# Reordering the matrix products of a decoder's attention passes on TensorE

## The chip, the cores and the metric
One core of a Trainium2 chip runs the whole kernel in one launch. The metric is the device time in microseconds (us), median of several executions. PE is TensorE (its weight loads are listed as PEld), DVE is VectorE, ACT is ScalarE, POOL is GpSimd, SP is the engine that issues the transfers, PSUM is the accumulator memory with eight banks of 128 x 512 words of 32 bits.

## What is computed
The input x is (2 sequences, 512 tokens, 128 channels). Six blocks follow, each `x = x + block(layernorm(x))`: attention (A), attention to a context with a top-32 choice (B), an FFN with 4-bit quantization (C), six layers of linear attention (D), attention to the context (E), and last six layers of local attention with an FFN (F), half of the kernel's time. Of F the reference says, cut to what matters:

```python
for i in range(6):
    x = attn_layer(shift_tokens(x), Wqkv[i], q_scale[i], k_scale[i], Wo[i]) + x
    x = ffn_layer(shift_tokens(x), ln_g[i], ln_b[i], W1[i], b1[i], W2[i], b2[i]) + x
# attn_layer: q, k, v = split(x @ Wqkv, 3), 16 heads of 64
#   q, k = l2norm(q) * qs, l2norm(k) * ksc; rotary tables on both
#   windows of 32: softmax(8 * q k^T, masked) v, each window sees itself and the one before
#   out @ Wo
# ffn_layer: layernorm; a, gate = split(xn @ W1 + b1, 2); (a * gelu(gate)) @ W2 + b2   (341 wide)
```

Block A has the same attention with one layer, its own mask width the same, and no l2 norm.

## The kernel before
Channels lie on the 128 partitions and the 512 tokens of a sequence along the free dimension, all in 32-bit floats. F is made of twelve units, one for each layer and sequence (b = 0, 1), and A of two. `attn_pe`, `attn_act`, `attn_dve`, `attn_pool` and `attn_sp` write the order of a unit out by hand, one for each engine; every engine works strictly in that order, and semaphores join them. A unit has three parts.

**Projection** (`a_head_pe`, `a_proj_pe`). The 16 heads are eight pairs p. For each, one product gives the queries (L285) and one the keys (L290), 128 x 512, into banks 0/1 and 2/3; ACT squares them (L485, L487), DVE multiplies them with the rotary tables (L603, L604, `a_rope_dve`), SP's transfers swap neighbouring partitions (L732), and POOL adds (L699, L700). Eight value products (L274, `a_v_pe`, i = 0 to 7) are spread over projection and first steps; ACT copies them out (L477). `a_ss_pe` (L329) sums squares for the l2 norm into bank 5. At the end ACT turns the sums into factors (guard L509, Ln L511, Exp L512), and two spreads (L337) bring the factors of pair 0 to all partitions, queries to bank 3 and keys to bank 2; those of the other pairs are bf16 products (L339). DVE multiplies the queries of a pair by its spread (`a_q_norm_dve`, L617; for pair 0 the keys too, L623); ACT copies the keys' spread (`a_k_norm_act`, L530) for POOL's multiply (L692).

**Steps** (`a_steps_pe`, p = 0 to 7). The mask is written into banks 0 and 1 by bf16 products (L370; L365 in step 7), the scores are added to it (L382), DVE takes maxima (L652) and subtracts (L655), ACT takes exponentials (L538), DVE sums the rows and inverts (L638, L645), POOL scales (L708), PE turns the result (L396, banks 4 and 5), ACT copies it out (L550), PE multiplies it with the values (L413, bank 6), ACT copies that out (L543), and the output product (L423) adds it up in bank 7. In the order of PE, step p has the mask and scores of p, the spreads of the queries of p+1 and the keys of p+2, the values of p-2, the turn of p-1 and the output product of p-3. ACT has in step p: copy of the key spread p+2, exponentials of p, merge of p-2, turned copies of p-1.

**Tail** (`a_tail_pe`). The last values, turn and output products, with the first products of the next unit's projection among them.

The FFN of a unit is done in the next unit's projection, through hooks by pair: `f_centre_pe` (L1886), `f_var_pe` (L1891), `f_up_pe` for i = 0, 1, 2 (gate L1899 in bank 6, up L1901 in bank 7), with i = 2 under the name "up", and `f_down_pe` (three products L1907, bank 7) under "down". ACT does the Gelu (L1957) and reloads the table of exponentials (L1961), DVE multiplies (`f_mul_dve`, L2003) and adds the result to x (L2008) after step 1. After step 3 DVE copies the shifted x, the source of the unit after the next, and in units of b = 1 it scales the rotary tables for the next layer (L2014) after step 5. `take(pe, k)` makes PE wait until bank k's last reader is done; `read` marks that. The last FFN has no next unit and runs alone at the end (`f_pe`).

## Time and profile before

| | us |
|---|---|
| median of 3 runs (lowest, highest) | 1825.26 (1824.89, 1825.85) |
| the profiled execution | 1826.93 |
| its span, first to last instruction | 1825.0 |
| busy: PE, DVE, ACT, POOL | 1598.0, 1211.4, 904.7, 583.9 |
| mean granted clock of PE, share of full speed | 0.938 |

The rows below are read so. A timeline row gives the start, the length from the first start to the last end, the engine and line, the operation, what it writes and reads, and how many instructions are merged; in brackets stand the time for which the engine had been idle and who released it. Products overlap at their ends, so the distance of two starts is the time that one takes from the engine. A 32-bit product of 128 x 512 is two instructions. A row of the table by stretches gives the busy time of each engine in a stretch. F runs from about 870 us to the end.

### The profile page before, as it was taken

Reading aid. Unit: us, or ns where it says so; the run is one execution under the profiler, and the core shown is the slowest. Engines: PE = TensorE matmul, PEld = TensorE weight load, DVE = VectorE, ACT = ScalarE, POOL = GpSimd, SP = SyncE. Lnnn points to the kernel's source line nnn. Section 1 sums busy time; section 2 is a strip of 40 time slices with the busy share of each in tenths; the row PEclk is TensorE's granted clock in tenths of the full one; section 3 lists DMA queues with packets and bytes.
Section 4 is the critical chain, followed back from the end, with each engine's and each line's share of the span. In section 5 each row is a group of like instructions: output and inputs, shape, how many; then the busy total and the mean of one; then the engine's idle time right before and its main releaser. Section 6 shows DMA issues by size and latency. Waiting matters only on the chain.

```text
span 1825.0 us, 37900 instructions
## 1 busy us (share of the span) xinstructions
PE 1598.0 (88%) x15445; PEld 865.5 (47%) x15445; DVE 1211.4 (66%) x2060; ACT 904.7 (50%) x1581; POOL 583.9 (32%) x546
## 2 busy tenths in 40 slices
PE   7877656999999998676899999999999999989996
PEld 2545324556556654221364454545546454453543
DVE  6685566556656564433777776877867787687773
ACT  2445322453444343223566566666666656656563
POOL 5461000000000000000556455465544646545461
PEclk9998567999999999677899999999999999999998
DMA  7130010000000000002313313142231422314120
GB/s 244 36 98 1 0 30 11 7 20 1 21 20 1 21 1 1 1 1 89 124 43 120 106 44 121 63 125 84 77 124 37 148 76 75 109 52 136 57 82 12
DMA packets 49514, 110.48 MB, mean 61 GB/s; under 512 B 15168, under 2 KB 20032, under 8 KB 48192
## 3 DMA queue, kind: packets, MB, share of 16 engines
q1 hardware_dynamic: 49344, 108.07, 18.2%
q8 instruction: 124, 2.03, 0.5%
q14 instruction: 46, 0.38, 0.1%
HBM read 28.61 MB, written 0.52 MB: 16 GB/s over the span
## 4 chain that ended last, share of the span: by engine, by line
PE 53%; DVE 27%; ACT 9%; issue 5%; DMA 2%; POOL 2%; SPq 1%; DVEq 0%; ACTq 0%
DVE nm L652 4%; PE ps L285 4%; PE ps L290 4%; DVE nm L638 3%; PE ps L1506 3%; PE ps L423 3%; PE ps L413 3%; PE ps L274 3%; PE ps L1557 3%; DVE big L655 2%; PE ps L1566 2%; PE ps L1525 2%; PE ps L396 2%; DMA big<-big 2%; DVE big L1750 2%
## 5 line engine op out<-in xcount | busy, mean ns | idle before, releaser
L699 POOL TENSOR_TENSOR big<-big 128x512 f32<-128x512 f32 x112 | 142.9, 1276 | 903.3 <-DMA big<-big 902.4
L708 POOL TENSOR_TENSOR big<-big,nm 128x384 f32<-128x384 f32 x224 | 189.4, 866 | 186.7 <-DVE nm L645 186.7
L603 DVE TENSOR_TENSOR big<-ps,big 128x512 f32<-128x512 f32 x224 | 153.7, 686 | 84.4 <-ACT sq L485 56.1
L538 ACT ACTIVATE big<-big 128x384 f32<-128x384 f32 x224 | 109.4, 522 | 126.1 <-DVE big L655 125.9
L604 DVE TENSOR_TENSOR big<-ps,big 128x512 f32<-128x512 f32 x224 | 152.6, 681 | 0.0
L413 PE MATMUL ps<-big 128*64 128x64 f32 x3584 | 129.1, 225 | 24.1 <-ACT big L550 23.8
L413 PEld LDWEIGHTS ps<-big 128*64 128x64 f32 x3584 | 115.1, 138 | 64.6 <-ACT big L550 47.5
L1750 DVE TENSOR_TENSOR big<-ps,fix 128x512 f32<-128x512 f32 x192 | 119.2, 683 | 36.4 <-PE ps L1506 36.0
L700 POOL TENSOR_TENSOR big<-big 128x512 f32<-128x512 f32 x112 | 143.1, 1277 | 0.0
L396 PE MATMUL ps<-ident,big 128*128 128x128 f32 x896 | 128.5, 282 | 14.5 <-POOL big L708 12.5
L692 POOL TENSOR_TENSOR big<-big 128x512 f32<-128x512 f32 x84 | 107.1, 1275 | 72.2 <-ACT big L530 72.1
L652 DVE TENSOR_REDUCE nm<-ps 128x4 f32<-128x384 f32 x224 | 112.2, 543 | 26.0 <-PE ps L382 23.5
L550 ACT ACTIVATE big<-ps 128x512 f32<-128x512 f32 x224 | 122.0, 593 | 9.4 <-PE ps L396 7.5
L477 ACT ACTIVATE big<-ps 128x512 f32<-128x512 f32 x112 | 66.6, 595 | 110.7 <-PE ps L274 110.7
L396 PEld LDWEIGHTS ps<-ident,big 128*128 128x128 f32 x896 | 96.8, 141 | 40.0 <-POOL big L708 26.9
L655 DVE TENSOR_TENSOR big<-ps,nm 128x384 f32<-128x384 f32 x224 | 113.5, 549 | 0.3
L638 DVE TENSOR_REDUCE nm<-big 128x8 f32<-128x768 f32 x96 | 91.5, 953 | 21.2 <-ACT big L538 19.5
L285 PE MATMUL ps<-xsh,big 128*128 128x512 f32 x192 | 101.6, 611 | 4.1 <-issue 4.1
L274 PE MATMUL ps<-big,xsh 128*128 128x512 f32 x192 | 103.9, 623 | 0.0
L382 PE MATMUL ps<-big 64*64 64x96 f32 (+1 forms) x3584 | 97.5, 244 | 5.8 <-DVE big L623 2.2
L423 PE MATMUL ps<-fix,big 128*128 128x512 f32 x192 | 99.6, 600 | 0.7 <-ACT fix L543 0.7
L290 PE MATMUL ps<-xsh,big 128*128 128x512 f32 x192 | 98.9, 597 | 0.0
(286 smaller groups left out, 2892.3 us busy)
## 6 DMA issues: line engine op xcount, KB each, us to landing
big<-big SPq DMA_DIRECT2D x224, 256.0 KB, 2.4
big<-big SPq DMA_DIRECT2D x112, 128.0 KB, 2.4
big<-in_F_w SPq DMA_DIRECT2D x6, 1536.0 KB, 6.7
big<-big SPq DMA_DIRECT2D x84, 64.0 KB, 2.0
big<-in_D_w SPq DMA_DIRECT2D x12, 256.0 KB, 2.9
big<-in_F_wo SPq DMA_DIRECT2D x6, 512.0 KB, 4.4
big<-in_F_w SPq DMA_DIRECT2D x6, 341.0 KB, 3.0
big<-in_A_w SPq DMA_DIRECT2D x1, 1536.0 KB, 11.1
```

The lines of the kernel that those rows point to most:

```text
L274: pe.matmul(ps[:, kv, :], src_of(key, b)[:, 128 * t:128 * t + 128], Wqkv[:, 2, 512 * hf:512 * hf + 512], start=True, stop=True).then_inc(* ...
L285: pe.matmul(ps[:, kq, :], Wqkv[:, 0, 128 * p:128 * p + 128], src_of(key, b), start=True, stop=True).then_inc(*full[kq].mark((key, b, "q", p)))
L290: pe.matmul(ps[:, kk, :], Wqkv[:, 1, 128 * p:128 * p + 128], src_of(key, b), start=True, stop=True).then_inc(*full[kk].mark((key, b, "k", p)))
L396: last = pe.transpose(ps[:, 4 + h, 128 * j:128 * j + 128], P[:, 2 * (p % 2) + h, at0:at0 + 128], ident[:, :])
L413: last = pe.matmul(ps[64 * h:64 * h + 64, 6, 64 * m:64 * m + 64], vv[:, m // 2, 128 * p + 64 * h:128 * p + 64 * h + 64], PT[:, 2 * (p % 2) ...
L423: last = pe.matmul(ps[:, Y, :], Wo[:, p, :], ot(key, p), start=p == 0, stop=p == NP - 1)
L603: dve.tensor_tensor(tmp[:, i, w, :], ps[:, k, :], tb[:, 2 * w, :], ALU.mult).then_inc(*part.mark((key, b, p, 0)))
L604: dve.tensor_tensor(sinp[:, i, T * w:T * w + T], ps[:, k, :], tb[:, 2 * w + 1, :], ALU.mult).then_inc(*part.mark((key, b, p, 1)))
L652: dve.tensor_reduce(nm[:, i, 4 * h:4 * h + 4], s4(h), AX, ALU.max).then_inc(*topped.mark((key, b, p, h)))
L655: dve.tensor_tensor(shft[:, 2 * (p % 2) + h, :].rearrange("p (j k) -> p j k", j=4), s4(h), nm[:, i, 4 * h:4 * h + 4].unsqueeze(2).to_broad ...
L708: pool.tensor_tensor(v, v, nm[:, p % 3, 16 + 4 * h:20 + 4 * h].unsqueeze(2).to_broadcast([128, 4, KW]), ALU.mult)\
L1750: dve.tensor_tensor(sT[:, ch % 2, r, :].rearrange("p (g i) -> p g i", g=4), ps[:, r, :].rearrange("p (g i) -> p g i", g=4), tri.unsqueeze( ...
```

## The change
PE's order is changed, and one bank; no product is added or removed, and ACT's, DVE's, POOL's and SP's orders stay. (1) `a_proj_pe`: the value product i = 5 goes ahead of the first two spreads, and the down products i = 0 and 1 behind them; the third down product goes into step 0. (2) `a_steps_pe`: the spreads stand between mask and scores from step 1 on (the key spreads of pairs 2 and 3 stay behind the value products of steps 0 and 1), and the hooks of a step ahead of those value products. (3) `a_tail_pe`: the next unit's first query product goes ahead of the values of pair 6, its first key product behind them, and the next two projections ahead of the output product of pair 6. (4) The third up product uses bank 2 in place of 7. Cut to its core:

```diff
@@ a_qk_pe is split: a_q_pe has the query product, a_k_pe the key product @@
+        def a_qk_pe(pe, key, b, p):
+            a_q_pe(pe, key, b, p)
+            a_k_pe(pe, key, b, p)
@@ a_proj_pe @@
                 a_ss_pe(pe, key, b, NP // 2 - 1)
-                a_v_pe(pe, key, b, 4)
+            a_v_pe(pe, key, b, 4)
+            a_v_pe(pe, key, b, 5)
+            if l2:
+                a_spread_q_pe(pe, key, b, 0)
+                a_spread_k_pe(pe, key, b, 0)
                 if "down" in hooks:
                     hooks["down"]()
-                a_spread_q_pe(pe, key, b, 0)
-                a_spread_k_pe(pe, key, b, 0)
-            else:
-                a_v_pe(pe, key, b, 4)
-            a_v_pe(pe, key, b, 5)
@@ a_steps_pe @@
                 a_mask_pe(pe, key, b, p, l2)
+                if l2 and p >= 2 and p + 2 < NP:
+                    a_spread_k_pe(pe, key, b, p + 2)
+                if l2 and 0 < p < NP - 1:
+                    a_spread_q_pe(pe, key, b, p + 1)
                 a_scores_pe(pe, key, b, p, l2)
-                if l2 and p + 1 < NP:
-                    a_spread_q_pe(pe, key, b, p + 1)
                 if l2 and p == 0:
+                    a_spread_q_pe(pe, key, b, 1)
                     a_spread_k_pe(pe, key, b, 1)
+                if p in late:
+                    late[p]()
                 if p < 2:
                     a_v_pe(pe, key, b, NT + 2 + p)
-                if l2 and p + 2 < NP:
-                    a_spread_k_pe(pe, key, b, p + 2)
-                if p in late:
-                    late[p]()
+                    if l2:
+                        a_spread_k_pe(pe, key, b, p + 2)
                 if p >= 2:
                     a_values_pe(pe, key, b, p - 2)
@@ a_tail_pe @@
+            if nxt:
+                a_q_pe(pe, *nxt, 0)
             a_values_pe(pe, key, b, NP - 2)
+            if nxt:
+                a_k_pe(pe, *nxt, 0)
             a_out_pe(pe, key, b, NP - 3)
-            if nxt:
-                a_qk_pe(pe, *nxt, 0)
             a_turn_pe(pe, key, b, NP - 1)
-            a_out_pe(pe, key, b, NP - 2)
             if nxt:
                 a_qk_pe(pe, *nxt, 1)
                 if v_with(l2, 1) is not None:
                     a_v_pe(pe, *nxt, v_with(l2, 1))
+            a_out_pe(pe, key, b, NP - 2)
             a_values_pe(pe, key, b, NP - 1)
@@ f_up_pe and f_mul_dve use bank UP[i] for the up product @@
+        UP = (7, 7, 2)
-            take(pe, 7)
-            pe.matmul(ps[0:m, 7, :], W1[:, c0:c0 + m], fxn, ...)
+            take(pe, UP[i])
+            pe.matmul(ps[0:m, UP[i], :], W1[:, c0:c0 + m], fxn, ...)
@@ f_down_pe @@
-        def f_down_pe(pe, l, b):
-            take(pe, Y)
-            for i, (c0, m) in enumerate(DIC):
+        def f_down_pe(pe, l, b, parts):
+            for i in parts:
+                if i == 0:
+                    take(pe, Y)
@@ f_pe_hooks: early, late (the epilogue calls f_down_pe with range(3)) @@
-                     "up": lambda: f_up_pe(pe, *u, 2), "down": lambda: f_down_pe(pe, *u)}, {})
+                     "up": lambda: f_up_pe(pe, *u, 2), "down": lambda: f_down_pe(pe, *u, (0, 1))}, {0: lambda: f_down_pe(pe, *u, (2,))})
```

## Rows read from the trace of the kernel before

**Rows 1.** The page, PE's busy tenths in 40 equal slices of the span
```profile
PE   7877656999999998676899999999999999989996
```
**Rows 2.** Table by stretches, one unit of each kind: stretch, length, busy by engine
```profile
1100.00:1177.00 77.00, 72.43 (x743) 37.98 (x742) 59.57 (x105) 48.04 (x85) 42.28 (x39) 1.00 0.29 95
1177.00:1255.00 78.00, 73.30 (x745) 38.35 (x744) 57.91 (x103) 48.50 (x86) 41.77 (x39) 1.00 0.27 88
```
**Rows 3.** PE's waits from 870 us on: total, times, longest
```profile
PE ps L413 <- ACT big L550: 19.9, 41, 1.1
PE ps L370 <- DVE big L655: 9.8, 22, 0.5
...
PE ps L1901 <- DVEq L136: 5.1, 5, 1.1
```
**Rows 4.** Timeline of PE, end of a projection and step 0, table unit
```profile
1129.50 2.74 PE L1907 MATMUL ps<-fix,big 128*128 128x512 f32 x6
1132.17 1.13 PE L337 MATMUL ps<-rs,big 32*128 32x512 f32 x4
...
1134.84 0.89 PE L382 MATMUL ps<-big 64*64 64x64 f32 x32 [0.20 <-DVE big L623]
...
1135.98 1.12 PE L274 MATMUL ps<-big,xsh 128*128 128x512 f32 x2
```
**Rows 5.** Timeline of ACT in the same unit
```profile
1128.87 0.69 ACT L509 ACTIVATE rs<-ps,eps 128x512 f32<-128x512 f32 x1
...
1130.43 0.72 ACT L512 ACTIVATE rs<-rs,eps 128x512 f32<-128x512 f32 x1
```
**Rows 6.** Timeline of PE, tail of the same unit, back-to-back products
```profile
1172.55 1.13 PE L423 MATMUL ps<-fix,big 128*128 128x512 f32 x2
1173.51 1.02 PE L285 MATMUL ps<-xsh,big 128*128 128x512 f32 x2
1174.37 1.02 PE L290 MATMUL ps<-xsh,big 128*128 128x512 f32 x2
```
**Rows 7.** Timeline of PE, step 4 of the table unit
```profile
1151.90 0.36 PE L370 MATMUL ps<-band,identb 64*64 64x384 bf16 x4
1152.09 0.83 PE L382 MATMUL ps<-big 64*64 64x64 f32 x32
1152.85 0.39 PE L339 MATMUL ps<-xn,big 32*128 32x512 bf16 x2
1153.16 1.15 PE L413 MATMUL ps<-big 128*64 128x64 f32 x32
```
**Rows 8.** Timeline of DVE in step 0 of the same unit
```profile
1135.76 1.02 DVE L652 TENSOR_REDUCE nm<-ps 128x4 f32<-128x384 f32 x2 [0.41 <-PE ps L382]
...
1139.31 0.95 DVE L638 TENSOR_REDUCE nm<-big 128x8 f32<-128x768 f32 x1 [1.00 <-ACT big L538]
```
**Rows 9.** Timelines of ACT and PE, end of a projection, plain unit
```profile
1207.56 0.69 ACT L509 ACTIVATE rs<-ps,eps 128x512 f32<-128x512 f32 x1 [1.13 <-PE ps L329]
...
1211.05 1.13 PE L337 MATMUL ps<-rs,big 32*128 32x512 f32 x4
```
**Rows 10.** Timelines of DVE and PE around step 3 of the table unit
```profile
1146.73 0.68 DVE L617 TENSOR_TENSOR big<-big,ps 128x512 f32<-128x512 f32 x1
...
1147.47 0.89 PE L382 MATMUL ps<-big 64*64 64x64 f32 x32
...
1148.51 0.97 DVE L652 TENSOR_REDUCE nm<-ps 128x4 f32<-128x384 f32 x2
```
**Rows 11.** Timeline of PE, values of pair 6, table and plain unit
```profile
1171.47 1.15 PE L413 MATMUL ps<-big 128*64 128x64 f32 x32 [0.67 <-ACT big L550]
...
1249.06 1.15 PE L413 MATMUL ps<-big 128*64 128x64 f32 x32 [1.13 <-ACT big L550]
```
**Rows 12.** Timelines of PE and DVE in the epilogue
```profile
1814.84 1.09 PE L1901 MATMUL ps<-xc,big 128*85 128x512 f32 x2
...
1816.83 2.84 PE L1907 MATMUL ps<-fix,big 128*128 128x512 f32 x6 [0.90 <-DVEq L136]
...
1819.71 0.75 DVE L2008 SCALAR_TENSOR_TENSOR x<-ps,big,x 128x512 f32<-128x512 f32 x1 [2.99 <-PE ps L1907]
```

More of the change, by code:

```diff
@@ L275, in a_v_pe, with a_q_pe @@
                       start=True, stop=True).then_inc(*full[kv].mark((key, b, "v", i)))
-        def a_qk_pe(pe, key, b, p):
-            kq, kk = p % 2, 2 + p % 2
+        def a_q_pe(pe, key, b, p):
             if p == 0:
@@ L281, in a_qk_pe, with a_k_pe @@
             if p < 2:
-                take(pe, kq)
+                take(pe, p)
             else:
                 pe.wait_ge(*q_part.at((key, b, p - 2, 1)))
-            pe.matmul(ps[:, kq, :], Wqkv[:, 0, 128 * p:128 * p + 128], src_of(key, b), start=True, stop=True).then_inc(*full[kq].mark((key, b, "q", p)))
+            pe.matmul(ps[:, p % 2, :], Wqkv[:, 0, 128 * p:128 * p + 128], src_of(key, b), start=True, stop=True).then_inc(*full[p % 2].mark((key, b, "q", p)))
+        def a_k_pe(pe, key, b, p):
+            kk = 2 + p % 2
             if p < 2:
@@ L1899, in f_up_pe @@
             pe.matmul(ps[0:m, 6, :], W1[:, DI + c0:DI + c0 + m], fxn, start=True, stop=True).then_inc(*full[6].mark(("F", l, b, "gate", i)))
[L1900 to L1905 removed]
+            take(pe, UP[i])
+            pe.matmul(ps[0:m, UP[i], :], W1[:, c0:c0 + m], fxn, start=True, stop=True).then_inc(*full[UP[i]].mark(("F", l, b, "up", i)))
+        def f_down_pe(pe, l, b, parts):
+            for i in parts:
+                if i == 0:
+                    take(pe, Y)
+                m = DIC[i][1]
                 pe.wait_ge(*f_mul.at((l, b, i)))
                 last = pe.matmul(ps[:, Y, :], W2[0:m, i, :], fh[0:m, i, :], start=i == 0, stop=i == 2)
[L1908 removed]
+            if i == 2:
+                last.then_inc(*full[Y].mark(("F", l, b, "f2")))
         def f_before(l, b):
@@ L1932, in f_pe @@
                 f_up_pe(pe, *u, i)
-            f_down_pe(pe, *u)
+            f_down_pe(pe, *u, range(3))
         def f_square_act(act, l, b):
@@ L2000, in f_mul_dve @@
             m = DIC[i][1]
-            dve.wait_ge(*full[7].at(("F", l, b, "up", i)))
+            dve.wait_ge(*full[UP[i]].at(("F", l, b, "up", i)))
             dve.wait_ge(*gg.at((l, b, i)))
-            dve.scalar_tensor_tensor(fh[0:m, i, :], ps[0:m, 7, :], b1[0:m, i:i + 1], fg[i % 2][0:m, :], ALU.add, ALU.mult).then_inc(*f_mul.mark((l, b, i)))
-            read(dve, 7, f_mul, (l, b, i))
+            dve.scalar_tensor_tensor(fh[0:m, i, :], ps[0:m, UP[i], :], b1[0:m, i:i + 1], fg[i % 2][0:m, :], ALU.add, ALU.mult).then_inc(*f_mul.mark((l, b, i)))
+            read(dve, UP[i], f_mul, (l, b, i))
         def f_add_dve(dve, l, b):
```

2 lines of the change are left out of this document (removed).

## The prediction
> **What bounds the kernel now.** I read the 40 slices of the page first: TensorE (PE) is at nine tenths or more in nearly every slice from the 21st on [rows 1], the last of the kernel's stages, which the change touches most. The table by stretches [rows 2] cuts that stage into its twelve units: 77 us for one of sequence 0 (a *plain* unit), 78 us for one of sequence 1 (a *table* unit, named for the scaling of the rotary table that VectorE does in it), with PE busy for 72.4 and 73.3. So at most some 4 to 5 us of each unit are waits of PE, about 50 us in all, and everything else that PE does is kept by the change. The list of PE's waits [rows 3] names them: the value products wait for ScalarE to bring the turned probabilities out of PSUM (19.9 us in 41 places), the masks for VectorE's subtraction (9.8), and 5 times the third "up" product of the FFN for a freed bank (5.1). Reading the timeline of one unit engine by engine then shows what sets the pace. The projection is a packed PE. In the steps it alternates: PE is packed in some of them, in a table unit VectorE has no gap from the row sum of step 0 to step 7, and ScalarE's evacuations pace the value products. That decides how to sum: an edit counts where it moves PE in the projection and the tail, and the row sum of step 0 in the steps.
>
> **Head of the steps.** Now: three down products, the two first spreads, the value product i=5, the mask, the scores [rows 4]. The spreads start at 1132.17 only because the down products (2.67 us) stand ahead of them; their operand is ready when ScalarE's exponential ends, 1130.43 + 0.72 = 1131.15 [rows 5]. In the new order product i=5 fills the time up to there (its bank is free at 1128.87 + 0.69 = 1129.56, and a product takes 0.86 [rows 6]), and the spreads start at 1131.2, 1.0 earlier. Behind them now stand 2.67 us to the scores, of which a wait for VectorE is about 0.35 (the mask alone takes 0.19 before unhindered scores [rows 7]). In the new order two down products take the place of one value product: 2.67 - 0.35 + 0.86 = 3.2. So the scores of step 0 start 0.5 earlier, and VectorE's first maximum with them.
>
> But the third down product, 0.86, now stands in step 0 ahead of value product i=6. ScalarE works in order: copy of i=6, copy of the second key spread, exponentials of step 0, and the row sum waits 1.00 for these [rows 8]; it comes 3.33 after the start of product i=6 (1135.98). So that product and the row sum come -0.5 + 0.86 = **0.4 later** in a table unit. VectorE had no gap from here on, so this is a loss, although PE itself has waits in this step that could hold the product: it fits PE's gaps but not ScalarE's queue.
>
> **Third up product in bank 2.** In the plain units of layers 1 to 5 it waits about 1.0 [rows 3]. Bank 2 was last read by the rotary multiply of pair 6, long before. Then the square sums come earlier, and ScalarE's guard activation, which idles 1.13 for them [rows 9], starts at 1206.43 after its table load. The spreads can follow 1131.2 - 1128.87 = 2.3 later, at 1208.8 instead of 1211.05: 2.3 earlier. With the same 0.5 and 0.86 behind them the row sum comes **0.9 earlier**. In table units nothing waited there.
>
> **Spreads behind the mask.** Work is moved, not removed: a pair of spreads takes 0.31, mask 0.19, scores 0.76 [rows 7]. The key spread can use the wait behind the mask. The query spread can't: it and the scores wait for the same VectorE multiply. In step 3 that ends at 1146.73 + 0.68 = 1147.41, and the scores start at 1147.47 [rows 10]; now the query spread's 0.31 comes between. The maxima of step 3 start at 1148.51 by VectorE; new by PE: 1147.47 + 0.4 + 0.31 + 0.92 = 1149.1 (0.92 from the start of scores to the maxima, [rows 4, 8]), so 0.2 more late than the 0.4. In steps 4 and 5 PE is packed, and the scores come 0.31 later against the same chain, while the values come no later. One more change of tile shape is added per step (mask, spread, scores; it was mask and scores together). [rows 6] give the nearest price: 0.96 from the output product, behind the values' other tile shape, to the query product, against 0.86 where the shape stays; so 0.10, between 0 (hidden, since the masks are short) and 0.2 (on either side); I take 0.10. No reason makes it a gain. Together the slip over the steps is 0.2 to 1.0; I take 0.6 in a table unit, where VectorE's table work hands the whole lateness on, and 0.35 in a plain unit, where PE gets the 0.31 back in step 6.
>
> The Trainium skill (TensorEngine Tiling (Array Packing), Key Properties) says that changing the tiling mode, not just the tile, drains TensorE. By this rule the extra changes are never free, and the trace agrees as far as it goes (0.96 against 0.86); no row shows a spread between mask and scores. Without it the sum would be about 1 us lower.
>
> **Tail.** The next unit's first query product, 0.86, goes ahead of the value product of pair 6, which waits 1.13 in a plain and 0.67 in a table unit [rows 11]. Its bank is free since VectorE's last subtraction (done before the output product ahead of it ends), its source since step 3. So it is hidden: **-0.86** plain, **-0.74** table (0.12 hangs over). The key product moved behind those values, the next queries ahead of the sixth output product: same work, and PE has no other wait there. Rotary work of pairs 0 and 1 starts earlier on VectorE, and SP issues these swaps earlier, but from pair 2 on it still follows the residual add. SP is passed no new DMA.
>
> **Last unit and epilogue.** It has no successor, so its tail keeps its wait: +0.4 + 0.35. In the epilogue the down products wait for the last multiply, since bank 7 is theirs and the third up product's: up at 1814.84, down at 1816.83, add at 1819.71 [rows 12]. With bank 2 the first two can start behind the up product, 1815.6; the third starts at 1817.3, and the add at 1818.4: **-1.3**.
>
> **The sum.** Five plain units with an FFN: 5 x (-0.9 + 0.35 - 0.86) = -7.0. Five table units: 5 x (0.4 + 0.6 - 0.74) = +1.3. First unit (no FFN, tail gain less slip) -0.5. Last unit +0.75. Epilogue -1.3. The first stage's tail is nearly without a wait: nothing. Sum -6.8. The profiled span is 1825.0 (that execution 1826.9); the median of the runs is 1825.26, so 1825.3 - 6.8 = **1818.5**.
>
> **Rivals.**
> *ScalarE's ring decides (slower).* The values of step p need the evacuation that ScalarE does behind the exponentials of step p-1. The new order puts the values right behind the scores, 0.31 closer, with 0.1 more for the tile shapes. If that ring is the bound in every step, two steps take 0.41 more, one 0.2, seven of them 1.4 per unit in place of my mean 0.5: 12 x 0.9 = +11, giving 1829.5. It decides from a slip of about 1.1 per unit (0.15 per step). For it: 41 waits on these evacuations; against: between them stand steps in which PE is packed without a wait (1151.90 to 1153.16 unbroken [rows 7]).
> *The freed bank is waited for again (no change).* The first key spread now stands behind the last FFN multiply, which reads bank 2. If that multiply comes late, the plain units lose their 1.3 again: 5 x 1.3 = 6.5, giving 1825. Against: even now, behind the wait of 1.0, that multiply is done before ScalarE's guard activation starts at 1207.56, and the spreads come later than 1208.
> *Everything fits the gaps (clearly faster).* If the third down product vanishes in step 0's gaps and no slip arises, 11 x 0.86 + 12 x 0.5 = 15 more: 1803. Against: ScalarE's order above.
> That the change doesn't do what it says holds for half of "spreads behind the mask" and is in the sum.
>
> **Chances.** Forecast 0.60, with its own range 1813 to 1823 (each term of a unit wrong by 0.4); ring 0.13; bank 0.14; all fits 0.13. The range takes in the forecast and the near half of the others: 1808 to 1828. A measurement can tell about 0.2% (3.7 us) from no change. Faster: 0.52 of the forecast and all of the last, 0.65. Same: 0.08 and the bank, with 0.01 of the ring: 0.23. Slower: 0.12.
>
> **What would show it.** Right: no wait of the third up product; the next query product ahead of the values of pair 6, and that wait gone or under 0.3; in step 0 VectorE's row sum waiting for ScalarE near 1.4 instead of 1.0; the query spread starting where VectorE's multiply ends. A plain and a table unit together, 155 now, near 153.9. Wrong: value products waiting 0.5 or more in most steps (ring), the first key spread waiting for VectorE (bank), or steps without PE waits at all.

## The result, and the profile after

| | before | after |
|---|---|---|
| median (lowest, highest) in the same session, us | 1826.23 (1824.5, 1829.32), 11 runs | 1831.06 (1827.59, 1840.46), 11 runs |
| ratio after to before | | 1.0036, 95% interval 1.0021 to 1.0050 |
| the profiled execution; its span | 1826.93; 1825.0 | 1828.03; 1826.2 |
| busy: PE, DVE, ACT, POOL | 1598.0, 1211.4, 904.7, 583.9 | 1611.0, 1224.9, 901.7, 584.9 |
| mean granted clock of PE | 0.938 | 0.935 |

The kernel became slower by 0.36%; 1818.5 was predicted, in a range of 1808 to 1828. It also became uneven: its runs spread over 13 us, those of before over 5. The profiled execution is one of the shortest of after: it lies 1.1 us above that of before, the medians lie 4.8 apart. In its code the two spreads of pair 0 are L342, the other spreads L344, the mask L375 (L370 in step 7), the scores L387, the turn L401, the values L418, the up product L1913, the down product L1921; on DVE the row sum is L648, the residual add L693, the shift copies L2002 and L2003.

**PE's waits** from 870 us on, after (compare [rows 3]):

```profile
PE ps L401 <- POOL big L718: 13.6, 11, 1.2
PE ps L418 <- ACT big L560: 8.5, 25, 1.0
PE ps L370 <- DVE big L665: 5.1, 5, 1.0
PE ps L342 <- ACT rs L522: 5.1, 12, 0.4
PE ps L375 <- DVE big L665: 3.7, 8, 0.5
...
PE ps L1896 <- DVE xsh L2003: 2.8, 5, 1.8
PE ps L387 <- DVE big L633: 1.8, 1, 1.8
...
PE ps L1913 <- DVEq L136: 0.4, 2, 0.2
```

The waits that the change aimed at are down: values 19.9 to 8.5, masks 9.8 to 3.7, third up product 5.1 to nothing (the 0.4 of the last line are waits of the second up product). Larger is the first line: 11 waits ahead of the turn of step 0, each of 1.24, where before has 0.52 (6.4 us in 12). But from 870 us to the end PE's idle time fell in all from 70.9 to 58.5 us, while its busy time grew by 13.6, from 884.1 to 897.7. So the list of waits doesn't show the loss, and the units have to be looked at one by one.

**Where the units changed.** The distance from the first spreads of one unit (L337 before, L342 after) to those of the next is a unit's period; it is read from the timeline of PE. *P* is the period from a plain unit to the table unit behind it (steps of the plain one, projection of the other), *T* the other one.

| period, us | before | after | the sum's working |
|---|---|---|---|
| first unit | 76.67 | 80.06 | 75.2 |
| T, five | 78.72 to 78.88 | 77.73 to 78.04 | 77.8 |
| P, five | 76.25 to 76.26 | 77.53 77.35 77.50 76.88 77.24 | 76.2 |
| last spread to the end | 72.66 | 71.56 | 73.1 |

The working is the sum's, cut at the spreads, which come 1.0 earlier in a table unit: so the first unit is 76.67 - 0.5 - 1.0, and the last stretch 72.66 + 0.75 + 1.0 - 1.3. The T periods came as worked out. The P periods are 5.5 us too long together, the first unit 4.9; these two make most of the error. The last stretch is 1.5 shorter, but it holds a piece at the lower clock in every trace, before's too (13.7 us there, 6.8 in after), so I take nothing from it.

**P periods: VectorE's copies.** Timelines of DVE and POOL in the tail of a plain unit, before:

```profile
1105.19 0.69 DVE L683 TENSOR_TENSOR x<-x,ps 128x512 f32<-128x512 f32 x1 [1.52 <-PE ps L423]
1106.02 0.42 DVE L1987 COPY xsh<-x 64x512 f32<-64x512 f32 x1
1106.48 0.42 DVE L1988 COPY xsh<-x 64x511 f32<-64x511 f32 x1
...
1106.67 1.37 POOL L699 TENSOR_TENSOR big<-big 128x512 f32<-128x512 f32 x1 [0.77 <-DMA big<-big]
```

and the same place after:

```profile
1107.35 0.69 DVE L693 TENSOR_TENSOR x<-x,ps 128x512 f32<-128x512 f32 x1 [2.25 <-PE ps L428]
1108.18 1.46 DVE L2002 COPY xsh<-x 64x512 f32<-64x512 f32 x1
1109.68 1.39 DVE L2003 COPY xsh<-x 64x511 f32<-64x511 f32 x1
...
1108.10 1.26 POOL L709 TENSOR_TENSOR big<-big 128x512 f32<-128x512 f32 x1 [0.75 <-DMA big<-big]
1109.33 1.46 POOL L710 TENSOR_TENSOR big<-big 128x512 f32<-128x512 f32 x1
...
1111.12 1.13 PE L1896 MATMUL ps<-xsh,fix 128*128 128x512 f32 x2 [0.24 <-DVE xsh L2003]
```

The copies take 1.46 and 1.39 in place of 0.42. It is so in three of the five P periods (77.53, 77.50, 77.24); in the other two the second copy alone is long, and the clock, below, has its part (77.35, 76.88). Before, the first copy started 0.65 ahead of POOL's rotary addition of the next unit's pair 1. Now VectorE's rotary work of pairs 0 and 1, which stands ahead of the residual add, is done 0.73 earlier against that add (DVE idles 2.25 before it in place of 1.52), the swaps and POOL's additions follow it, and POOL starts 0.08 *ahead* of the copy (0.65 - 0.73). Each copy then waits for the addition under way to end; the second addition, 1.46, waits in turn. PE's product L1896 is fed by the second copy. The Trainium skill (SBUF — State Buffer, SBUF: two separate sides) says that VectorE in a two-port mode and GpSimd arbitrate for one shared port pair, which is an exclusive lock held for the whole instruction; the trace agrees, with 0.42 against 1.39 to 1.46.

The kernel before already has such a pair in every unit behind the first, after step 3, where GpSimd's scaling starts 0.16 behind the first copy:

```profile
1152.11 0.37 DVE L1987 COPY xsh<-x 64x512 f32<-64x512 f32 x1
1152.51 0.94 DVE L1988 COPY xsh<-x 64x511 f32<-64x511 f32 x1
...
1152.27 1.86 POOL L708 TENSOR_TENSOR big<-big,nm 128x384 f32<-128x384 f32 x2 [0.75 <-DVE nm L645]
```

The second copy takes 0.94 in place of 0.42. The prediction had no row of it.

**The clock.** Table by stretches around step 0 of a plain unit, after; the last three columns are granted clock, DMA share, GB/s:

```profile
1215.00:1222.00 7.00, 6.85 (x85) 2.97 (x83) 4.43 (x9) 3.20 (x7) 2.54 (x2) 1.00 0.36 78
1222.00:1225.00 3.00, 1.78 (x14) 1.05 (x14) 3.00 (x7) 2.25 (x6) 2.79 (x3) 0.94 0.22 46
1225.00:1228.00 3.00, 3.00 (x56) 2.46 (x56) 2.41 (x6) 1.01 (x2) 2.25 (x4) 0.50 0.19 35
```

and PE there:

```profile
1223.09 1.44 PE L401 MATMUL ps<-ident,big 128*128 128x128 f32 x8 [1.24 <-POOL big L718]
1224.46 0.38 PE L375 MATMUL ps<-band,identb 64*64 64x384 bf16 x4
1224.78 0.61 PE L344 MATMUL ps<-xn,big 32*128 32x512 bf16 x2
1225.31 1.56 PE L387 MATMUL ps<-big 64*64 64x64 f32 x32
1226.80 1.71 PE L418 MATMUL ps<-big 128*64 128x64 f32 x32
```

Some 1.6 us after the end of the wait of 1.24 the clock falls to 0.50 of full speed, 1.2 GHz in place of 2.4, for 3.4 us, and 32 score products take 1.56 where they take 0.89 at full clock. This happened in three of after's eleven such units, one of them the last; in before, where this wait is 0.52, in none. In the first unit of after, which has no down products to put behind its first spreads, the same is larger. Timeline of PE:

```profile
899.14 1.13 PE L342 MATMUL ps<-rs,big 32*128 32x512 f32 x4 [0.42 <-ACT rs L522]
900.20 0.36 PE L375 MATMUL ps<-band,identb 64*64 64x384 bf16 x4
902.35 0.89 PE L387 MATMUL ps<-big 64*64 64x64 f32 x32 [1.79 <-DVE big L633]
904.08 0.70 PE L344 MATMUL ps<-xn,big 32*128 32x512 bf16 x2 [0.84 <-DVE xn L642]
904.72 2.07 PE L274 MATMUL ps<-big,xsh 128*128 128x512 f32 x2
```

The value product i=5, which filled the wait for VectorE, now stands ahead of the spreads. PE idles 1.79 and 0.84, and its clock is low from 903.8 to 914.1; before, only from 901.7 to 905.1.

### The profile page after: what moved, and what is told of

Its sections match the earlier page's. It is cut to its first block, busy times and chain, and to the rows that moved or that the text cites. A ratio compares the mean times of both kernels' runs of the same rounds, so it can differ in the third digit from the quotient of the medians.

```text
span 1826.2 us, 37900 instructions
## 1 busy us (share of the span) xinstructions
PE 1611.0 (88%) x15445; PEld 869.0 (48%) x15445; DVE 1224.9 (67%) x2060; ACT 901.7 (49%) x1581; POOL 584.9 (32%) x546
## 4 chain that ended last, share of the span: by engine, by line
PE 60%; DVE 20%; ACT 12%; issue 5%; POOL 2%; DMA 1%; SPq 0%; DVEq 0%; ACTq 0%; POOLq 0%
PE ps L292 4%; PE ps L418 4%; PE ps L284 4%; PE ps L428 4%; PE ps L401 3%; PE ps L1516 3%; DVE nm L662 3%; PE ps L274 3%; PE ps L1567 3%; PE ps L387 2%; PE ps L1576 2%; PE ps L1535 2%; PE ps L1921 2%; DVE big L1760 2%; PE ps L1911 2%
## 5 line engine op out<-in xcount | busy, mean ns | idle before, releaser
L613 DVE TENSOR_TENSOR big<-ps,big 128x512 f32<-128x512 f32 x224 | 153.8, 687 | 76.9 <-ACT sq L495 39.3
L548 ACT ACTIVATE big<-big 128x384 f32<-128x384 f32 x224 | 109.8, 522 | 159.3 <-DVE big L665 159.2
L401 PE MATMUL ps<-ident,big 128*128 128x128 f32 x896 | 127.4, 283 | 21.5 <-POOL big L718 19.7
L418 PE MATMUL ps<-big 128*64 128x64 f32 x3584 | 131.2, 227 | 13.5 <-ACT big L560 12.4
L418 PEld LDWEIGHTS ps<-big 128*64 128x64 f32 x3584 | 117.1, 140 | 47.7 <-ACT big L560 31.3
L401 PEld LDWEIGHTS ps<-ident,big 128*128 128x128 f32 x896 | 97.8, 142 | 44.9 <-POOL big L718 30.7
L487 ACT ACTIVATE big<-ps 128x512 f32<-128x512 f32 x112 | 66.4, 593 | 103.0 <-PE ps L274 103.0
L648 DVE TENSOR_REDUCE nm<-big 128x8 f32<-128x768 f32 x96 | 91.5, 953 | 33.4 <-ACT big L548 31.6
L387 PE MATMUL ps<-big 64*64 64x96 f32 (+1 forms) x3584 | 101.6, 250 | 1.9 <-DVE big L633 1.8
```

The source lines that it names most:

```text
L401: last = pe.transpose(ps[:, 4 + h, 128 * j:128 * j + 128], P[:, 2 * (p % 2) + h, at0:at0 + 128], ident[:, :])
L418: last = pe.matmul(ps[64 * h:64 * h + 64, 6, 64 * m:64 * m + 64], vv[:, m // 2, 128 * p + 64 * h:128 * p + 64 * h + 64], PT[:, 2 * (p % 2) ...
L613: dve.tensor_tensor(tmp[:, i, w, :], ps[:, k, :], tb[:, 2 * w, :], ALU.mult).then_inc(*part.mark((key, b, p, 0)))
```

## The experiments

Each ratio is to the kernel before on the same chip, with its 95% interval. Where a kernel has "additions", the shift in the tail is made by two additions from PSUM in place of the copies (those after step 3 stay). T and P are the periods of the profiled execution after the first unit. Since such a kernel's time scatters with the collisions, I read the time and the periods together. Each of the four groups below has its own runs of before: medians 1823.47, 1826.92, 1825.01 and 1826.48, the first two on one chip. So two ratios of one group compare well; the difference of two from different groups may be off by some 0.2%. Every trace has 3.4 to 13.7 us at the lower clock in the epilogue, and the last stretch is 68.2 to 73.0; no edit is behind this.

| kernel | ratio (95%) | P | T | wait ahead of the turn, total |
|---|---|---|---|---|
| after, again | 1.0076 (1.0060, 1.0091) | 76.2 to 78.0 | 77.7 to 80.5 | 13.6 |
| after, v5 late in first unit | 1.0075 (1.0060, 1.0090) | 76.5 to 77.9 | 78.6 to 81.0 | 14.5 |
| after, additions | 1.0030 (1.0019, 1.0042) | 76.1 to 76.8 | 78.0 to 79.8 | 13.6 |
| after, old tail | 1.0052 (1.0039, 1.0065) | 76.98 | 78.5 (one 79.0) | 13.7 |
| before, additions | 1.0003 (0.9994, 1.0012) | 76.26 | 79.2 to 79.4 | 6.5 |
| before, new tail | 1.0011 (1.0001, 1.0021) | 75.4, later 77.7, 78.2 | 78.0, later 79.0, 81.4 | 6.5 |
| before, new tail, additions | 0.9978 (0.9969, 0.9987) | 75.40 (one 76.2) | 78.6 (one 79.8) | 6.5 |
| the same with the freed bank | 0.9943 (0.9931, 0.9955) | 75.39 | 77.2 (one 78.2) | 6.4 |
| the same with the new head: all but the steps | **0.9912 (0.9900, 0.9924)** | 75.0 to 75.3 | 76.9 to 77.3 | 4.5 |
| all but the head, additions | 0.9972 (0.9962, 0.9982) | 75.8 to 76.1 | 77.7 to 78.7 | 6.6 |
| all, v5 late, additions | 0.9988 (0.9979, 0.9997) | 76.2 to 77.4 | 78.2 to 79.3 | 14.5 |
| the same, third down product in the head | 0.9988 (0.9980, 0.9997) | 76.12 (one 76.4) | 78.1 to 79.7 | 6.5 |
| the same, third down product behind i=6 | 0.9961 (0.9947, 0.9975) | 75.61 | 78.1 to 78.8 | 2.9 |
| after, third down product behind i=6 | 1.0019 (1.0007, 1.0031) | 75.67 | 77.9 to 80.4 | 2.1 |
| all but the steps, with the copies | 0.9952 (0.9940, 0.9965) | 75.04 or 76.17 | 77.3 or 79.1 to 79.4 | 4.5 |

### First group: the copies, the first unit, the tail

The kernel after unchanged, for the others to be compared with:

> The changed kernel once more, as it is: how its runs scatter, and whether what its first trace showed comes again. If the trace of the changed kernel is typical, this one has again the long shift copies on VectorE in the plain units' tails (1.4 us each in place of 0.42) and the low clock around 903 to 914 us, a ratio near 1.002 to 1.005, and units of 77.3 and 77.7 us. If the scatter of its runs (1827.6 to 1840.5, against 1824.5 to 1829.3 before) comes from the granted clock, this trace shows more or longer stretches at 1.2 GHz when its time is high. Rival: the scatter is the chip's own and the kernel before shows as much on the same chip.

1838.58 (1833.12 to 1839.12), ratio 1.0076. The kernel after has no single time: in this profile both copies are long in some *table* tails too (at 1188 and 1499), and just there the T periods are 80.00 and 80.45 in place of 78.

The value product i=5 behind the spreads again, in the unit without down products alone:

```diff
-            a_v_pe(pe, key, b, 5)
+            if not l2 or "down" in hooks:
+                a_v_pe(pe, key, b, 5)
             ...
                 if "down" in hooks:
                     hooks["down"]()
+                else:
+                    a_v_pe(pe, key, b, 5)
```

> The changed kernel, but in the first unit, which has no FFN work, value product i=5 goes back behind the first spreads. Theory (clock): without down products the changed order leaves TensorE idle for 1.8 and 0.8 us around the first scores, the granted clock falls to 1.2 GHz for some 10 us (903 to 914), and the first unit is 3.4 us longer than before (80.1 against 76.7 from spread to spread). Filled again, the first unit takes 76 to 77 and the whole is about 3 us shorter than the changed kernel. Rival: the low clock stems from what lies before it (the stage boundary), and comes whatever stands there; then under 1 us.

1837.5, ratio 1.0075. The first unit is 76.94 in place of 78.64 (80.06 in the first profile), so the mechanism is there; in the time it can't be seen, since the collisions scatter by more. For the time this run is inconclusive.

The shift without copies. The source x + y is read from PSUM, where the output product adds up y; nothing is left out:

```diff
@@ cut: the waits and marks are left out @@
+  dve.tensor_tensor(xsh[0:64, b, :], x[0:64, T*b:T*b + T], ps[0:64, Y, :], ALU.add)
+  dve.tensor_tensor(xsh[64:128, b, 1:T], x[64:128, T*b:T*b + T - 1], ps[64:128, Y, 0:T - 1], ALU.add)
-            late[NP + 2] = lambda: f_shift_dve(dve, l, b)
```

> The changed kernel, but VectorE makes the shifted x behind the tail as two additions from PSUM and x (both 0.69 us) in place of two copies within SBUF (0.42 alone, 1.4 when GpSimd adds at the time). The value is the same. Theory (collision): the changed tail brings GpSimd's rotary adds under these copies in plain units, two copies cost 2.0 us more there, and TensorE gets about 1 us of it as waits in the next projection. Without copies no collision: VectorE's part is 1.4 in every unit, against 0.84 undisturbed and 2.9 disturbed; the plain units take 76.3 to 76.8 from spread to spread, the table units 77.7 to 78.2, and the whole is 2 to 5 us shorter than the changed kernel. Rival: TensorE's own order (spreads, tile shapes) makes the plain units long; then no gain, or a loss of 0.5 us per unit.

1828.99, ratio 1.003, 9.6 us under the kernel after on the same chip, where I had expected 2 to 5. The undisturbed P periods are 76.14 and 76.17, what the sum's working gave. T is 78.0 to 79.8; two of the long ones hold a fall of the clock to 1.2 GHz, a third (79.03) a wait of 0.79 of the second up product. So the copies are a cause, not the only one. The edit does two things: the shift reads PSUM, and it stands ahead of the residual add, some 0.8 earlier. No kernel has one without the other. That an operation with a PSUM operand isn't stopped is seen in VectorE's rotary multiplies: they take 0.68 with a GpSimd addition under way (1260.47 and 1260.24 in the last kernel of the fourth group).

The kernel after with the old tail:

```diff
-            if nxt:
-                a_q_pe(pe, *nxt, 0)
             a_values_pe(pe, key, b, NP - 2)
             ... (the rest of a_tail_pe as before)
```

> The changed kernel with the tail of before (next query product behind the values of pair 6, next queries behind the output product). By the sum of the prediction the tail gave 0.86 and 0.74 per unit, so this should be about 9 us slower than the changed kernel. Theory (collision): it takes the collision away with the gain, since the first two rotary passes and their swaps come later again; then VectorE's shift copies are 0.42 long, and it is slower by only 0.8 x 11 - 1.0 x 6 = 3 us or less.

1833.12, ratio 1.0052, *less* than the kernel after in this group (1.0076), though not than its first result (1.0036). All its tail copies take 0.42, and P is an even 76.98. In after the new tail thus loses through the copies about what it gains, here more. But 1.0052 is well over 1: something else in the change costs as well.

### Second group: the tail on the kernel before

The control, before with the additions:

> The kernel before, with its two shift copies replaced by two additions that read the down sum from PSUM (0.69 us each instead of 0.42; nothing is left out). It is the control for the kernels that have the same edit. Collision theory: in the kernel before the copies run free (0.42 us) in the tails, so nothing is won; ratio to before 0.999 to 1.001. Rival, that the form of the shift is worth something by itself whatever the order of the passes: 0.995 or less, the same 9 us that it gave on the kernel after.

Ratio 1.0003: the form of the shift is worth nothing by itself (T is even 0.4 longer, since an addition takes 0.69 and a copy 0.42).

Before with the new tail alone (only `a_tail_pe` and the split of `a_qk_pe`):

> The kernel before with the new tail alone (query product of the next unit ahead of the late values). Collision theory: the 0.86 us per unit that the tail's working gives are there, but the copies of the plain units rise from 0.42 to about 1.4 us and give about 1.1 us back in those units; 1818 to 1824, ratio 0.997 to 1.000, plain-to-table periods no shorter than 76.3. Rival, head and steps are what made the kernel slower and the tail is clean: both kinds of period fall by 0.8, 1815, ratio 0.9955.

Ratio 1.0011. I had expected at most 1.000. The first unit has both copies long (78.15 in place of 76.67). Behind it P is 75.4 and T 78.0, 0.86 and 0.8 less than before, with the tail copies at 0.42 but for the second one in two P periods (1.38 and 1.40), which costs nothing there. From 1489 us on both copies are long in three of the last four tails that have a successor (1.38 to 1.48 and 1.39), in the third of the four the second alone, and the periods go up to 81.35, 78.19, 78.95, 77.66. One and the same program gains 0.8 in a unit or loses 2, by which of two engines comes first.

The same with the additions:

> The kernel before with the new tail, and with the shift as two additions from PSUM, so that no copy is there to be stopped. Collision theory: the tail's 0.74 to 0.86 us per unit arrive whole, periods 75.5 and 78.1, about 8 us in all: 1815 to 1817, ratio 0.9955. Rival, that the new order of the tail costs elsewhere (a PSUM bank, ScalarE, the residual add): same as before, ratio 1.0.

1823.97, ratio 0.9978. P is 75.40, by 0.86 under the control's 76.26, to the hundredth what the tail's working gave; T falls by 0.7. The gain in time, 0.25% of 1827 or 4.6 us against the control, is smaller than the 7.8 of the undisturbed periods; a wait of 1.4 of the second up product in one unit (T 79.80), one of 0.58 in the next and a longer slow stretch at the end (13.7 us in place of 6.8) take some of it.

The kernel after with both suspected causes taken away:

> The kernel after with both suspected causes taken away: the shift as two additions from PSUM, and in the first unit, which has no down products, the last value product back behind the spreads. If the two causes add, it lies 1.6 to 3 us under the kernel with the shift alone (ratio 1.003): 1821 to 1824, ratio 0.999 to 1.001, first unit 76.9 instead of 78.5. Rival, the first unit's slow clock is paid by something else: ratio stays 1.003. What neither covers is step 0's single wait of 1.24 us ahead of the turn (0.52 before): if a long wait there lets the clock fall, some units stay at 79.5 with granted clock 0.98 and others at 78.0 with 1.00.

1825.55, ratio 0.9988; first unit 75.71. Still four units in which the clock falls, each behind the wait of 1.24. The ratio is 0.42% under that of the additions alone, the median 3.4 us, the first unit 2.8 (78.50 before): the rest of the 0.42% lies in the two groups' runs of before. The tail alone on the kernel before does no worse (0.9978). So head, bank and steps together, without a collision, gave *nothing*, where I had expected gains from the head and the bank. Two long T periods (79.30, 79.05) have no fall of the clock but a wait of 1.29 and 1.04 of the second up product; the fourth group comes back to it.

### Third group: which part of head, bank and steps

New tail and freed bank, head and steps as before, additions:

```diff
-        UP = (7, 7, 7)
+        UP = (7, 7, 2)
```

> The kernel before with the new tail, the freed bank for the third up product, and the shift as two additions from PSUM; head and steps as before. If the bank removes the waits of the third up product (9.1 us over F with the tail and the shift alone, ratio 0.9978) and nothing takes their place, 1816 to 1819, ratio 0.994 to 0.996. If the down products wait in its place, 0.9978 stays. Step 0's wait ahead of the turn stays 0.52 us, and no unit after the first shows a granted clock of 0.98.

1814.26, ratio 0.9943. T falls from 78.55 to 77.20, which is the 1.3 that I had worked out for the bank.

All but the head (old steps' counterpart):

> The kernel after with the old head (all three down products ahead of the spreads, last value product behind them) and the shift as two additions; steps, tail and bank are new. Theory that the third down product in step 0 lengthens what stands between the scores of pair 0 and those of pair 1, and so makes one wait of 1.24 us ahead of the turn after which the clock falls: here the wait is 0.5 to 0.8 us, no unit shows 0.98, 1819 to 1822, ratio 0.996 to 0.998. Rival, the new order of the steps makes the wait: it stays at 1.2 and some units show 0.98, ratio 0.999 to 1.001.

1820.5, ratio 0.9972. The wait ahead of the turn is 0.52, no clock fall: as the theory had it. But the new steps cost 0.29% against the kernel above (P 0.4 to 0.7 and T 0.5 to 0.8 longer, but for one T).

All but the steps. The order of `a_steps_pe` is that of before, the third down product is in step 0 as in after, but by that old order it stands *behind* the value product i=6 and the key spread:

> The counterpart: new head with the third down product in step 0, old order of the steps, last value product of the first unit behind the spreads, shift as two additions, new tail and bank. Theory that the head makes the long wait: it is 1.2 us or more here as well, some units show a granted clock of 0.98 and are 1.5 us longer, 1823 to 1826, ratio 0.998 to 1.000. Rival, the steps make it: wait of 0.5 to 0.8, no such unit, ratio 0.995 to 0.997.

1809.85, ratio 0.9912, P 75.02, no clock fall after the first unit. Waits of 1.24 are gone here as well, so neither the new head nor the new steps makes them alone: it takes the third down product in step 0 *and* an order that puts it ahead of i=6. The expected size was wrong too: this is the fastest kernel of the study, 15 us under before (1825.01 on that chip).

Third down product back in the head, all else as in the kernel with 0.9988:

```diff
-  "down": lambda: f_down_pe(pe, *u, (0, 1))}, {0: lambda: f_down_pe(pe, *u, (2,))})
+  "down": lambda: f_down_pe(pe, *u, (0, 1, 2))}, {})
```

> Both causes taken away as in the kernel with ratio 0.9988, and the third down product back in the head with the other two, so that step 0 has 0.86 us less to fill its wait. Theory that the clock falls by chance after a long single wait: the wait ahead of the turn rises from 1.24 to about 1.6 to 2.1 us and more units show 0.98 than the four of that kernel; the head is 0.86 longer, the wait 0.86 longer only if the scores of pair 1 do not move; 1826 to 1832, ratio 1.000 to 1.003. Rival, the wait follows the scores of pair 1, which come 0.86 earlier after the spreads: the wait stays 1.24 or falls, and the time stays at 0.9988 or under it.

Ratio 0.9988 again. I had expected the wait to grow; it fell to 0.52, with another of 0.43 ahead of the mask of pair 1, and the turn comes 10.58 behind the first spreads as in the other kernel. The step waits about the same time in either place; only its cut into one wait or two differs. One fall of the clock is left, in step 7, and the ratio is no better though the four behind the turn are gone.

What stands between the orders shows on ACT and DVE. Step 0 of a plain unit in the kernel with 0.9988, timelines of ACT and DVE (here L490 is the copy of value product i=6, L551 the exponentials, L651 the row sum):

```profile
1213.92 0.60 ACT L490 ACTIVATE big<-ps 128x512 f32<-128x512 f32 x1 [1.29 <-PE ps L274]
1214.63 0.60 ACT L543 ACTIVATE big<-ps 128x512 f32<-128x512 f32 x1
1215.13 0.93 ACT L551 ACTIVATE big<-big 128x384 f32<-128x384 f32 x2
...
1216.09 0.95 DVE L651 TENSOR_REDUCE nm<-big 128x8 f32<-128x768 f32 x1 [1.86 <-ACT big L551]
```

and in the one with 0.9912 (L487, L548, L648):

```profile
1208.43 0.60 ACT L487 ACTIVATE big<-ps 128x512 f32<-128x512 f32 x1 [0.43 <-PE ps L274]
1209.14 0.60 ACT L540 ACTIVATE big<-ps 128x512 f32<-128x512 f32 x1
1209.63 0.93 ACT L548 ACTIVATE big<-big 128x384 f32<-128x384 f32 x2
...
1210.59 0.95 DVE L648 TENSOR_REDUCE nm<-big 128x8 f32<-128x768 f32 x1 [1.00 <-ACT big L548]
```

ACT waits for the value product (1.29 against 0.43), the exponentials queue behind that copy, the row sum behind them: 0.86 all the way, the time of the third down product.

### Fourth group: the third down product, the spreads, the copies

The edit to `a_steps_pe`, in both of the first two kernels:

```diff
-                if p in late:
-                    late[p]()
                 if p < 2:
                     a_v_pe(pe, key, b, NT + 2 + p)
                     if l2:
                         a_spread_k_pe(pe, key, b, p + 2)
+                if p in late:
+                    late[p]()
```

> As the kernel with both suspected causes taken away (0.9988), and in step 0 the third down product behind the value product i=6 and its key spread instead of ahead of them; the steps keep the spreads behind the mask. Theory that ScalarE's order carries the third down product into the row sum: its copy of product i=6 starts 0.86 earlier, the row sum's wait falls from 1.86 to about 1.0 us, PE's single wait ahead of the turn from 1.24 to 0.3 to 0.5, no unit shows a granted clock of 0.98, and 11 times 0.87 go: 1811 to 1815, ratio 0.992 to 0.9945. Rival, it is the spreads behind the mask that cost (0.9988 against 0.9912 of the kernel with the old steps): 0.997 to 0.9988, with the wait's length changed or not.

1819.38, ratio 0.9961, between the two theories. PE's waits ahead of the turn, over all of F:

```profile
PE ps L404 <- POOL big L726: 2.9, 12, 0.9
```

The waits there fall from 14.5 to 2.9 in all, the clock never falls between the first and the last unit, and P goes from 76.18 to 75.61. So the place of the third down product is worth 0.27%, 5 us. The rest, 0.9961 against 0.9912, is the spreads behind the mask: 9 us. P is 0.59 longer for them and T 1.2, and PE's busy time in a P period is 73.70 in place of 72.66. Where it goes is seen in a step in which PE never waits, here step 4 of after (compare [rows 7]):

```profile
1155.78 0.36 PE L375 MATMUL ps<-band,identb 64*64 64x384 bf16 x4
1156.07 0.39 PE L344 MATMUL ps<-xn,big 32*128 32x512 bf16 x2
1156.39 0.89 PE L387 MATMUL ps<-big 64*64 64x64 f32 x32
1157.21 1.15 PE L418 MATMUL ps<-big 128*64 128x64 f32 x32
```

From the mask to the values it is 1.43 in place of 1.26: 0.10 more at the mask (0.29 for 0.19) and 0.06 more at the scores (0.82 for 0.76). Six steps have this, so my estimate is 1.0 of busy time, which is the 1.04. The lateness against the first spreads adds up, 0.16 at the values of step 2, 0.33 at those of step 4, 0.58 at those of step 6, and that is the 0.59 of P. In a T period VectorE hands on 0.8 at step 7's mask, and the other 0.4 is the second up product, which waits 0.67 in place of 0.21.

> The kernel after with that one move alone (third down product behind the value product i=6); the copies on VectorE stay, the first unit stays as in the kernel after. If ScalarE's order is a term of the loss beside the copies, about 9 us go of the 6 to 14 that after lies above before: 1821 to 1828, ratio 0.997 to 1.001, with the copies still at 1.4 us in the plain tails and some units 2 us longer for it. If the copies decide alone, it stays at 1.004 to 1.008.

1829.62, ratio 1.0019. That is between my two expectations (up to 1.001, from 1.004). It gives something to the kernel after as well, and P is an even 75.67. The T periods split cleanly: 80.24, 80.44, 80.18 where both copies are long, 77.94 and 78.24 where both are free.

All but the steps with the two copies of before (edit of the third group, without the additions):

> The kernel with ratio 0.9912 (old steps, new head, tail and bank, first unit's last value product behind the spreads), but with the shift as the two copies of the kernel before. It prices the stopped copies on a base that is otherwise clean: collision theory, copies of 1.4 us in the plain tails and in some table tails, 6 to 12 us more than with the additions, ratio 0.995 to 0.998. Rival, on this base the copies meet no addition of GpSimd: 0.991, and then the additions from PSUM are not needed.

1819.17, ratio 0.9952. That prices the collision: 0.40%, 7.3 us. Timeline of DVE in two table tails, the first free, the second stopped:

```profile
1334.79 0.42 DVE L2002 COPY xsh<-x 64x512 f32<-64x512 f32 x1
1335.25 0.42 DVE L2003 COPY xsh<-x 64x511 f32<-64x511 f32 x1
...
1488.30 1.39 DVE L2002 COPY xsh<-x 64x512 f32<-64x512 f32 x1
1489.73 1.39 DVE L2003 COPY xsh<-x 64x511 f32<-64x511 f32 x1
```

T is 77.3 with the free pair and 79.4 with the stopped one, 2.1 more; P is 75.04 and 76.17, 1.1 more. In a P period with the stopped pair PE's product L1896 and the query and key products behind it start 0.34, 0.69 and 1.03 later against the spreads. In a T period half of the price comes another way, as PE's second up product shows in the same two units:

```profile
1353.57 1.12 PE L1913 MATMUL ps<-xc,big 128*128 128x512 f32 x2 [0.62 <-DVEq L136]
...
1509.15 1.13 PE L1913 MATMUL ps<-xc,big 128*128 128x512 f32 x2 [1.65 <-DVEq L136]
```

It waits for bank 7, which VectorE's multiply of the first one frees, and that multiply stands in VectorE's queue behind rotary work which waits for GpSimd's additions (2.44 in the second unit, 1.56 in the first). So this wait is 1.4 to 1.9 in ten of the eleven T periods with a stopped pair. In the kernels with additions it is there too, 0.8 to 1.6 in their long T periods without a fall of the clock, but for one of 77.27 (0.59). In *late_behind* each P period has only the second copy long (1.38) and is 75.67, against 75.61 with the additions: in P one stopped copy fits, two do not. In T it need not fit: 78.95 for 78.0 in the new tail alone.

## Why the prediction was wrong

**The step that failed** is the sentence on the tail, "Rotary work of pairs 0 and 1 starts earlier on VectorE, and SP issues these swaps earlier, but from pair 2 on it still follows the residual add". It was true and priced at nothing. I followed the earlier work on VectorE and SP and not on to the engine behind them: POOL's additions moved 0.73 earlier against the residual add, into copies that had stood 0.65 ahead of them. Copies of 0.42 became 1.4, P periods grew by 1.1 and T periods by 2.1 where both were stopped. Priced on the clean base it is 7.3 us; on the kernel after, the additions gave back 8 to 10. With this alone, 1818.5 would have been about 1826 to 1828, 3 to 5 us under the measured 1831.06; the terms that follow make up the rest.

**The clock** had no term. A unit's waits were summed as PE time, as if 1.24 in one piece cost what 0.52 and others cost in several. In the six traces with the wait of 1.24 in every unit behind the first (after twice, additions, v5 late, old tail, all with v5 late and additions) the clock fell to 1.2 GHz 1.5 to 2.2 us behind its end, 17 times in 66, and for 3.4 us each time; behind step 7's waits of 1.03 and 0.57 it fell three times in all seventeen traces; in the eleven others, where the wait of step 0 is 0.9 or less, it never fell behind it. Most periods with a fall are 0.5 to 1.5 us longer, an estimate of 1 to 5 us in a run. The times don't show it by themselves: four falls less gave the same 0.9988. The first unit is the second case: I wrote "First unit (no FFN, tail gain less slip) -0.5" and didn't ask what fills the wait for VectorE there once i=5 is gone. Nothing does; the traces show 1.7 to 3.4 us more than 76.7 to 76.9, and the two kernels with additions that differ by this product alone 78.50 and 75.71.

**What held.** Tail: -0.86 plain against 0.86 measured, -0.74 table against 0.7 (on the kernels without copies). Bank: 1.3 worked out, 1.35 measured, and its wait is gone. Row sum in a table unit of after: 8.43 behind the first spreads in place of 7.14, while the spreads start 1.0 earlier against ACT's factors, so 0.3 later where I had 0.4. Its wait is 1.86, and I wrote 1.4. That was a slip in my own terms: with VectorE 0.5 earlier and the row sum 0.4 later the wait of 1.00 becomes 1.9. T in after: 77.74 against 77.8. Epilogue: the down products follow the up product without a wait, and the add comes 3.63 behind that product in place of 4.87, 1.24 earlier where I had 1.3.

**Where the mechanism was right and a size was off.** The spreads behind the mask cost 9 us (0.49%), and I had 0.6 and 0.35 per unit for the slip, some 5 us. On the clean base the P period grew by 0.59 and T by 1.2. My 0.10 for the change of tile shape held at the mask (0.29 for 0.19), but the scores then take 0.06 more as well, so a step costs 0.16 to 0.17; and in T I had no term for the second up product's 0.4. With the old head the same spreads cost 0.29%, so this price depends on what stands around them. The third down product ahead of i=6 I had at 0.86 less the 0.5 from the earlier scores. As a step by itself it costs 0.57 in a P period, and 5 us in all; it was a loss that moving one line avoids. The rule of the prediction that ScalarE's queue carries it on held exactly (0.86 at the copy, at the exponentials and at the row sum).

**The rivals.** ScalarE's ring, forecast at 1829.5, has the right time and the wrong mechanism: the waits on its evacuations fell from 19.9 to 8.5. The freed bank waited for again: no, neither the third up product nor the first key spread waits for it. Everything fits the gaps: it would have been near the truth for another change, the one without the new steps (1809.85). The slower side at 0.12 was too small: I had priced the moves on PE and left out what moves with them.

**Balance** of the parts: new tail -0.25%, freed bank -0.35%, new head -0.31%, spreads behind the mask +0.49%, third down product ahead of i=6 +0.27%, copies stopped +0.40% or more. The first five are steps of one chain, from the control at 1.0003 to 0.9988, so it is no proof that they sum to that difference; of the six only the tail and the head are differences within one group. The copies' price depends on the kernel: 0.40% here, 0.46% on after, and 1.0075 against 0.9988 (12 us) on the kernel with v5 late. With 0.40% the sum is +0.25%, and the first unit's 1.7 to 3.4 us add 0.1 to 0.2: about 0.4%, against the measured 0.36 and 0.76. How many tails collide in an execution differs from one to the next, and I take it, without a test of its own, for the distance of these two.

What decides in a given tail is when the swap of the next unit's pair 1 lands. In the six traces with the new tail and copies GpSimd waits for it 0.73 to 0.77 where both copies are stopped (its addition starts 0.06 to 0.16 ahead of the first), 0.83 to 1.12 where the second alone is (0.01 to 0.30 behind the first), and 1.5 to 3.0 where neither is (0.6 or more behind). Why the landing varies so stays open. That the clock falls in some units and not in others with the same wait stays open too.

## What to carry to other kernels

When an edit makes an engine's work earlier, follow it to the last engine of its chain, and look at what runs there now beside VectorE's copies: here a copy between SBUF tensors was stopped when a GpSimd addition was under way at its start, and 0.7 us of earlier work brought that about; the additions that read PSUM never were. Count what stands on PE ahead of each product that another engine copies out in order, since here a product put ahead of it was paid by all that queued behind that copy. And look at the longest single wait, not only at the total: gathered into one, the same waits can cost the clock.

## What the hardware showed that I had not expected

- A VectorE copy of 64 x 512 words in SBUF takes 0.42 us alone and 1.37 to 1.48 with a GpSimd addition of 1.26 under it, and the addition up to 1.54. The additions that read PSUM took 0.68 (64 x 512) and 0.69 (64 x 511) in all twelve tails of all nine kernels that have them.
- The granted clock fell to half 1.5 to 2.2 us behind a single wait of 1.24 us in 17 of 66 units, and came back 3.4 us later; with a wait of 0.52 in the same place it did not fall.
- Spreads of another tile shape between mask and scores add 0.10 behind the mask (0.29 against 0.19) and 0.06 behind the scores (0.82 against 0.76).
